# Weights split once in the first feed-forward part and reloaded as pairs, in a macaron block with a gated delta-rule attention

## The reference, cut to what matters

```python
x = x + 0.5 * ffn(layernorm(x))      # gate, up: 256 -> 768 (weights rounded to fp8), silu(gate)*up, down
x = x + attn(layernorm(x))
x = x + 0.5 * ffn(layernorm(x))

# attn: 16 heads of 128
q, k, v = silu(causal_conv4(x @ Wq)), silu(causal_conv4(x @ Wk)) * D**-0.5, silu(causal_conv4(x @ Wv))
alpha, beta = sigmoid(x @ Wa + ba), sigmoid(x @ Wb + bb)
def step(St, inp):                    # a scan over the tokens, per sequence and head
    q_, k_, v_, a_, b_ = inp
    err = einsum('bhij,bhj->bhi', St, k_) - v_
    Sn = a_ * St - b_ * err[..., None] * k_[..., None, :]
    return Sn, einsum('bhij,bhj->bhi', Sn, q_)
o = layernorm_per_head(scan(step)) * sigmoid(x @ Wg)
return o @ Wo
```

## Time and profile before

| | us |
|---|---|
| median of 3 runs | 2517.75 (2517.43 to 2521.06) |
| profiled execution, its own time | 2518.65 |
| its span, first to last instruction | 2516.9 |

### The profile page before, as it was taken

One profiled execution on the slowest core, in us unless ns is written; L12 is line 12 of the kernel. 1 busy time (PEld: TensorE's weight loads), 2 busy tenths in 40 slices (PEclk: granted clock), 3 DMA queues, 4 the chain that ended last, 5 costly groups with the idle time before them and its releaser, 6 DMA issues. The chain is left out here.

```text
span 2516.9 us, 64448 instructions
## 1 busy us (share of the span) xinstructions
PE 2364.4 (94%) x24496; PEld 1831.7 (73%) x24496; DVE 1989.7 (79%) x4226; ACT 1847.1 (73%) x3707; POOL 1873.3 (74%) x2057
## 2 busy tenths in 40 slices
PE   4996899999999999999998999999989999998598
PEld 2553688888777788888787888887778888887365
DVE  5654888888888788888887888888878888886353
ACT  2773677777888677777886777778867777776364
POOL 7762677777787777777886777778877777777365
PEclk8998999999999999999999999999999999999699
DMA  5000011111121111111211111112111111111001
GB/s 141 22 15 8 27 31 31 31 31 31 39 56 31 31 31 31 31 31 37 52 46 27 32 31 31 31 31 48 40 39 30 30 30 30 29 31 31 21 26 43
DMA packets 80609, 87.87 MB, mean 35 GB/s; under 512 B 21936, under 2 KB 50608, under 8 KB 80176
## 3 DMA queue, kind: packets, MB, share of 16 engines
q1 hardware_dynamic: 80304, 83.75, 13.9%
HBM read 77.83 MB, written 5.90 MB: 33 GB/s over the span
## 5 line engine op out<-in xcount | busy, mean ns | idle before, releaser
L1532 PE MATMUL a_bank<-k_z,k_kqv 128*128 128x512 f16 x2304 | 600.2, 381 | 11.2 <-DVE a_qb L1097 4.2
L1211 ACT ACTIVATE a_inv<-a_bank 128x512 f16<-128x512 f32 x640 | 382.9, 598 | 213.0 <-PE a_bank L1381 197.7
L1028 DVE TENSOR_TENSOR k_y<-a_bank,k_masks 128x256 f16<-128x256 f32 x768 | 318.5, 415 | 133.0 <-PE a_bank L1367 128.6
L1532 PEld LDWEIGHTS a_bank<-k_z,k_kqv 128*128 128x128 f16 x2304 | 198.5, 98 | 141.8 <-issue 19.5
L1097 DVE SCALAR_TENSOR_TENSOR a_kb<-a_bank,k_prm,a_kb 128x511 f32<-128x511 f32 (+2 forms) x384 | 282.8, 736 | 15.4 <-ACT a_kb L1155 15.0
L860 POOL TENSOR_TENSOR k_diag<-k_ident,k_bcol 128x512 f32<-128x512 f32 x128 | 133.0, 1039 | 215.0 <-DVE a_prod L1004 199.2
L1097 DVE SCALAR_TENSOR_TENSOR a_vb<-a_bank,k_prm,a_vb 128x511 f32<-128x511 f32 (+2 forms) x384 | 283.2, 738 | 0.1
L1097 DVE SCALAR_TENSOR_TENSOR a_qb<-a_bank,k_prm,a_qb 128x511 f32<-128x511 f32 (+2 forms) x384 | 282.4, 736 | 0.5
L1381 PE MATMUL a_bank<-a_inv,k_y 128*128 128x64 f16 x3072 | 272.0, 193 | 1.0 <-DVE k_y L1028 1.0
L1367 PEld LDWEIGHTS a_bank<-a_inv,a_am 128*128 128x128 f16 x3072 | 167.1, 98 | 105.8 <-ACT a_inv L1211 20.3
L1379 PE MATMUL a_bank<-k_y,a_inv 128*128 128x64 f16 x2560 | 236.6, 193 | 4.1 <-DVE k_y L1028 2.2
(11 more groups left out here) (151 smaller groups left out, 6778.3 us busy)
## 6 DMA issues: line engine op xcount, KB each, us to landing
a_decay<-decay_rows SPq DMA_DIRECT2D x128, 258.0 KB, 4.1
a_cum<-cumulative_rows SPq DMA_DIRECT2D x96, 258.0 KB, 3.6
stream<-in_L_attn_x SPq DMA_DIRECT2D x8, 512.0 KB, 6.8
out<-stream SPq DMA_DIRECT2D x8, 512.0 KB, 2.9
k_raw<-in_L_attn_Wk SPq DMA_DIRECT2D x16, 128.0 KB, 3.5
k_raw<-in_L_attn_Wq SPq DMA_DIRECT2D x16, 128.0 KB, 2.2
k_raw<-in_L_attn_Wv SPq DMA_DIRECT2D x16, 128.0 KB, 2.3
k_raw<-in_L_attn_Wg SPq DMA_DIRECT2D x16, 128.0 KB, 2.5
```

The costliest lines, as they stand in the source:

```text
L1028: nc.vector.tensor_tensor(even(y16[:, j], mb), bank[LEV[par]][:, 0:U * C // 2].rearrange("p (u b m) -> p u b m", u=U, m=mb), masks[:, j].r ...
L1211: nc.scalar.activation(both, bank[LEV[par]][:, :].rearrange("p (two b m) -> p two b m", two=2, m=mb), ACT.Copy).then_inc(m[f"act_lev{par}" ...
L1532: mm = pe.matmul(bank[PJ[j % 2]][:, :], wt, z16[:, zh, k, cols], start=(x == 0), stop=(x == 5))
```

## The change

All 16 heads' weights are split in the first feed-forward part. A part is now one kind of weight of one group, 128x1024 float32 (512 KB): 5 kinds times 4 groups are 20 parts, three in a turn from turn 1 on (`part_of`). SP loads a part into one of four raw buffers, ACT scales and rounds it in one instruction (`part_high`), DVE makes the low half in one (`part_low`). The parts of group 0 go straight to the tiles that the projections read; the other 15 go to one of two pair buffers, from which SP stores them to DRAM (`save_part`). In the attention the jobs are gone from ACT and POOL: SP loads a kind's pair, 512 KB, in one DMA each, five for a group, once the last projection with the old weights of that kind is done (`load_pairs`). Wo has two buffers, so its load does not wait for the last output. PE waits for the loads.

In the first feed-forward part the attention constants stand after turn 0 and the levels after turns 1 to 6, one in each (`level_constants`), both on POOL. ACT's turn begins four `silu` later, with the first ones ahead of the loop; DVE takes the statistics earlier and `hidden(b, 1)` into the turn; on PE `decay_products` stands earlier in the next turn, `strengths_turned` and `z_turned(1)` ahead of `down(b, 1)`, and `gate(b, 5)` after it. `root` counts on one semaphore in place of two. The last feed-forward part is as before but for that.

```diff
-JOBS = 4 * U + U
-SLOTS = 4
-WO_SLOTS = 1
-JOB_STEPS = {0: (0, 1, 2), 1: (3, 4, 5), 2: (6, 7, 8), 3: (9, 10, 11), 4: (12, 13, 14), 5: (15,)}
-OUT_STEPS = {8: (16, 17, 18, 19)}
-FIRST_JOB_STEP = -25
+KINDS = 5
+PARTS = KINDS * HG
+PART = KT * U * D
+RAW = 4
+PER_TURN = 3
+WO_SLOTS = 2
...
@@ first part: SP
+            def save_part(x):
+                if x is None:
+                    return
+                sp.wait_ge(d_part, x + 1)
+                if x >= KINDS:
+                    sp.dma_start(w_pairs[x], pairs[:, x % 2]).then_inc(s_pair[x % 2], 16)
+                if x + RAW < PARTS:
+                    load_part(x + RAW)
...
+                for x in range(RAW):
+                    load_part(x)
...
-                for job in range(6):
-                    load_job(nc, kit, w, sp, job)
-                for b in range(B):
-                    g = b % 2
-                    for job in range(3 * b + 6, min(3 * b + 9, JOBS)):
-                        load_job(nc, kit, w, sp, job)
-                    sp.wait_ge(d_ab, b + 1)
...
+                for t in range(1, B + 2):
+                    save_part(part_of(t, 0))
+                    store_rows(t - 2)
+                    save_part(part_of(t, 1))
+                    save_part(part_of(t, 2))
...
@@ first part: POOL
             def turn1(b):
                 low(b, 0)
                 root(1, b - 1)
                 low(b, 1)
-                weights(b, 0)
                 low(b, 2)
                 low(b, 3)
-                weights(b, 1)
+                root(0, b + 2)
                 low(b, 4)
                 low(b, 5)
-                root(0, b + 2)
-                weights(b, 2)
                 added(b)
...
                 root(0, 0)
-                attention_constants()
                 root(0, 1)
-                for b in range(0, B + 1):
+                for b in range(0, B + 2):
                     turn1(b)
+                    if b == 0:
+                        attention_constants()
+                    level_constants(b - 1)
...
@@ first part: DVE
+            def part_low(b, k):
+                x = part_of(b, k)
+                if x is None:
+                    return
+                dve.wait_ge(a_part, x + 1)
+                nc.vector.scalar_tensor_tensor(out=part_pair(x)[:, 1], in0=raw[:, x % RAW], scalar=WS,
+                                               in1=part_pair(x)[:, 0], op0=ALU.mult, op1=ALU.subtract)\
+                    .then_inc(d_part, 1)
...
             def turn1(b):
+                hidden(b, 1)
+                stats(1, b - 1)
                 hidden(b, 2)
+                part_low(b, 0)
+                hidden(b, 3)
                 logistic(b - 2)
+                stats(0, b + 2)
+                hidden(b, 4)
                 cumulative(b - 2)
-                hidden(b, 3)
                 strengths(b - 2)
-                hidden(b, 4)
                 low(1, b - 1)
                 hidden(b, 5)
-                stats(0, b + 2)
+                part_low(b, 1)
                 low(0, b + 1)
                 added(b)
+                part_low(b, 2)
                 hidden(b + 1, 0)
-                hidden(b + 1, 1)
-                stats(1, b)
...
@@ first part: ACT
+            def part_high(b, k):
+                x = part_of(b, k)
+                if x is None:
+                    return
+                act.wait_ge(s_part[x % RAW], 16 * (x // RAW + 1))
+                if x >= KINDS + 2:
+                    act.wait_ge(s_pair[x % 2], 16 * len(range(KINDS + (x - KINDS) % 2, x, 2)))
+                nc.scalar.activation(part_pair(x)[:, 0], raw[:, x % RAW], ACT.Copy, scale=WS).then_inc(a_part, 1)
...
             def turn1(b):
-                decays(b - 2)
-                silu(b, 0)
-                weights(b, 0)
-                silu(b, 1)
-                hidden_high(b, 0)
-                silu(b, 2)
-                normed(0, b + 1)
-                hidden_high(b, 1)
-                silu(b, 3)
-                hidden_high(b, 2)
-                weights(b, 1)
-                normed(1, b - 1)
                 silu(b, 4)
                 hidden_high(b, 3)
-                weights(b, 2)
                 high(1, b - 1)
+                hidden_high(b, 4)
                 silu(b, 5)
-                hidden_high(b, 4)
+                part_high(b, 2)
                 hidden_high(b, 5)
                 high(0, b + 1)
+                part_high(b + 1, 0)
+                normed(0, b + 2)
+                silu(b + 1, 0)
+                silu(b + 1, 1)
+                hidden_high(b + 1, 0)
+                part_high(b + 1, 1)
+                silu(b + 1, 2)
+                hidden_high(b + 1, 1)
+                silu(b + 1, 3)
+                hidden_high(b + 1, 2)
+                decays(b - 1)
+                normed(1, b)
...
+                normed(0, 1)
             act.wait_ge(s_small, 16 * (7 if first else 3))
             if first:
                 act.wait_ge(s_const, 8)
+            if first:
+                silu(0, 0)
+                silu(0, 1)
+                hidden_high(0, 0)
+                silu(0, 2)
+                hidden_high(0, 1)
+                silu(0, 3)
+                hidden_high(0, 2)
...
@@ first part: PE
                 gate(b, 3)
+                decay_products(b - 2)
                 up(b, 3)
+                gate(b, 4)
                 down(b, 0)
-                gate(b, 4)
                 up(b, 4)
+                strengths_turned(b - 2)
+                z_turned(1, b - 1)
+                down(b, 1)
                 gate(b, 5)
-                z_turned(1, b - 1)
-                strengths_turned(b - 2)
-                down(b, 1)
                 up(b, 5)
                 down(b, 2)
                 z_turned(0, b + 1)
-                decay_products(b - 1)
...
@@ attention: SP
+            def load_pairs(s):
+                group, kind = divmod(s - NC * (B - 1) + 2, NC * B)
+                group += 1
+                if kind >= KINDS or not 0 < group < HG:
+                    return
+                x = KINDS * group + kind
+                if kind < KINDS - 1:
+                    for j in range(U):
+                        sp.wait_ge(m[f"pe_pj{j}"], NC * (B * group - 1) + kind + 1)
+                else:
+                    need(sp, m["pe_wo"], NC * B * (group - WO_SLOTS + 1))
+                need(sp, m["dma_pairs"], 16 * (x - KINDS))
+                sp.dma_start(pair_tiles(kit, x), w_pairs[x]).then_inc(m["dma_pairs"], 16)
...
-                for job in jobs_of(s + 1) + jobs_of(s + 1, OUT_STEPS):
-                    load_job(nc, kit, w, sp, job)
+                load_pairs(s)
...
@@ attention: POOL and ACT
-            def weights(s):
-                for job in jobs_of(s - 2) + jobs_of(s - 1, OUT_STEPS):
-                    low_job(nc, kit, pool, job)
...
-                weights(s)
...
-            def weights(s):
-                for job in jobs_of(s - 1) + jobs_of(s - 1, OUT_STEPS):
...
@@ attention: PE
-                    pe.wait_ge(kit["pool_wl"], JOBS * (group + 1))
+                    need(pe, m["dma_pairs"], 16 * KINDS * group)
...
-                    if n % B == 0:
-                        pe.wait_ge(kit["pool_wl"], JOBS * (n // B) + U * i + j + 1)
+                    if n % B == 0 and j == 0 and n:
+                        pe.wait_ge(m["dma_pairs"], 16 * (KINDS * (n // B - 1) + i + 1))
...
-                    wt = gate16[:, wh, j, k] if i == 3 else kqv16[:, wh, i, j, k]
+                    wt = gate16[:, wh, k, j] if i == 3 else kqv16[:, wh, i, k, j]```

The order that follows from it, at three places. First ACT from its first silu (L528 before, L581 after) to the end of the products of turn 0; `f_sg` is the silu, `f_hh` the high half of the hidden values, `f_ztok` the normalised tokens, `k_raw` a weight tile. Before:

```order
5 L528 ACTIVATE f_sg<-f_bank,f_gs 128x512
6 L1623 ACTIVATE k_raw<-k_raw 128x256
7 L1625 ACTIVATE k_kqv<-k_raw 128x256
8 L528 ACTIVATE f_sg<-f_bank,f_gs 128x512
9 L537 ACTIVATE f_hh<-f_hid 128x512
10 L528 ACTIVATE f_sg<-f_bank,f_gs 128x512
11 L508 ACTIVATE f_ztok<-stream,f_shift,f_rstd 128x256 x4
12 L537 ACTIVATE f_hh<-f_hid 128x512
```

143 lines of the change are left out of this document (62 added, 81 removed).

## The result

The changed kernel takes 2474.37 us (median of 4 runs, 2473.62 to 2475.66), the kernel before, beside it, 2519.40 (2517.43 to 2521.45): a ratio of 0.9829, 95% interval 0.9817 to 0.984. The forecast was 2464.3, the range 2455 to 2475, so the result lies just inside its upper edge. The sign and the larger term were right; some 10 us were not won, and they are the subject of what follows. The profiled execution took 2475.66 us with a span of 2473.9.

What follows compares the result with a forecast made beforehand. The attention was taken as bound by PE except at three changes of group, which the weight jobs hold up. 2518.65 - 45.9 - (10 - 2.5 + 0) = 2465.2, with the median 0.9 lower: 2464.3 us, range 2455 to 2475.

Steps and rivals of the forecast that it cites:

- The attention, 45.9 us: Attention: removing the jobs wins the steps' whole excess, 45.9 us over 97 steps, 33.2 of it in three Wo steps.
- Loads of pairs, 0 us: Attention: 15 added loads of 512 KB land well inside over 25 us of room, so 0 is charged.
- Startup, 10 us won: First part, turn 0: it ends at 53.7 where it ended near 63.6, 10 us won.
- Turn 1, 23.4 us: First part: POOL's small constants make turn 1 take 23.4 us for 20.9, 2.5 us lost; bounds 0 and 5.
- Turns 2 to 7, 0 us: First part: six turns take 127.1 us in place of 127.2, 0 us; bounds -7 and +8.
- the one sentence on DVE: Turns 2 to 7: DVE's added 3 x 1.2 us stand in a turn with 8 us free, but ahead of the first `hidden`.
- the level on POOL: Turns 2 to 7: a level of 3.0 us for three jobs of 2.0, ahead of the root `normed(1)` waits for.
- The wait for stores, 1.4 us a turn in 4 to 6: First part: `part_high` waits for the store two parts back, 1.4 us of PE in each of turns 4 to 7; bounds 0 and 3.
- The rival "gives nothing back", 2472: First part: each `part_low` shuts POOL out for 1.2 us, six turns cost 7.5, startup's gain is gone: 2472; chance 0.2.
- One reading of the rows: Startup: four copies of a level took 4.71 us beside DVE's passes over two SBUF tensors, 1.14 us without them.

Runs made afterwards that it cites:

- the wait put back alone: Changed kernel with only POOL's wait for ACT put back in three steps, no work added: steps of 22.49, 23.0 and 23.27 us, 2494.7 us in the whole.
- low halves zero: Changed kernel with DVE writing zeros to each weight part's low half instead of subtracting: turns 2 to 7 126.0 us, whole 2464.95 us.
- the one with three buffers: Changed kernel with low halves written as zeros, and three pair and three raw buffers: turns 2 to 7 120.6 us, whole 2456.02 us.
- the three kernels with blocks of zeros: Changed kernel with zeros for the subtraction: written once 2464.95 us, written three times 2470.42 us, once with three pair and raw buffers 2456.02 us.
- the reordered kernel: Changed kernel with small constants before the first turn, third subtraction ahead of the scaling, levels' masks moved: 2466.15 us, ratio 0.9796.

## Why the prediction was right in the attention and wrong in the first part

- *The attention, 45.9 us:* measured 45.1 over the same 97 steps. Every step across a change of group is 16.0. The mechanism (the scaled q behind POOL's wait) holds by the wait put back alone.
- *Loads of pairs, 0 us:* they land in 4.7 to 6.0 us (medians by kind), and PE waits for none.
- *Startup, 10 us won:* 11.4, by the mechanism told: the first low half at 38.51 for 51.12. The sum had PE at the lower clock for 6 us from 37.85; it rose to 1.00 at 40.5, and with those 2.7 us the same sum ends turn 0 at 52.5 (measured: 52.37); with the rise at 43.6 (low halves zero) turn 0 ends at 53.74, nearly as forecast.
- *Turn 1, 23.4 us:* 24.1, but 22.6 at the full clock, so 1.7 us were lost against the 20.9 before, in place of 2.5. The cause was right: PE's two waits behind POOL make 4.6 of the 5.5 us charged, and the constants moved away take 3.2 us off. That 24.1 is so near to 23.4 is luck.
- *Turns 2 to 7, 0 us:* **this step failed**: 10.1 us lost, 11.7 at the full clock. The forecast of 20.7, 20.7, 21.7, 21.7, 21.7, 20.6 matches, nearly turn by turn, the kernel whose subtraction is a write of zeros: 20.3, 20.3, 21.7, 22.3, 21.7, 19.7. The term mis-sized most is the one sentence on DVE. Three times 1.2 us "in a turn that has 8 us free" were priced by the idle time of the whole turn. The subtractions stand in front of `hidden` and beside the root, and there they cost 11.3 us with their collisions. The second is the level on POOL, 3.0 us for jobs of 2.0, which got no time of its own in the sum though it "stands ahead of the root": without the levels the turns are 6.3 us shorter. The two costs overlap, since together they exceed the loss, and no run leaves out both.
- *The wait for stores, 1.4 us a turn in 4 to 6:* 1.6, 2.2 and 1.6 where the rest is out of the way (the zero kernel against the one with three buffers), and nothing where it is not.
- *The rival "gives nothing back", 2472:* this is what came. It charged six turns with 1.2 us each; they cost 1.7, and nearly 2 at the full clock. It had the rule right: the Trainium skill, "SBUF — State Buffer", section "Who interferes with whom", has GpSimd's reads shut out by a DVE instruction with two SBUF inputs but not by one with fewer, outside the modes in which it uses both ports. The trace agrees: L324, 0.20 us alone, takes up to 1.85 beside the subtraction and, in the first part, at most 0.49 in the three kernels with blocks of zeros. One reading of the rows was too wide: of the four copies that took 4.71 us in the kernel before, only one stood beside a pass over two tensors (1.73 us, from 25.72); the other three stood beside passes over one tensor and took 0.93 each, where undisturbed all four took 1.14. I gave it 0.2 on the ground that POOL was idle for 6 us a turn, which is again a share of a whole turn used for a question of place.
- *What two executions of one kernel differ by:* the places that differ by 1.4 to 1.7 us, in the turns, between the first and the fourth `a_at`, and at the end of the attention (2255.8 to 2259.1 us in the changed kernel), are stretches with the granted clock at 0.50. Why the clock falls behind one wait and not behind the same wait in another execution stays open.

## What to carry to other kernels

Work put on an engine with idle time is not free: ask which instruction it is queued ahead of, and what the other engine is doing at that moment. An instruction of 0.2 us on the path of a norm can pay for a whole subtraction elsewhere, and the row shows that as busy time, so compare its least and its most. Before a difference of 1 or 2 us is put down to an edit, compare the granted clock of the stretch. A wait whose removal gains nothing may only be hidden: here the buffers gained only once the order was mended. And a wait in an in-order queue is priced by what stands behind it: some 6 us of waiting on POOL, without work, cost 6.5 to 7.2 us a step, the lower clock behind it included.

## What the runs showed of the hardware that was not expected

POOL's steps are not the only ones to be held. DVE's scan over two SBUF tensors of 516 columns takes 1.21 us at the least (in the zero kernel) and 2.08 in the turn shown, begun beside POOL's low half at 137.98; and DVE's one-input L448 of the reordered kernel (L445 in the changed one, 32 x 512, f32 in place), otherwise 0.40 us, takes 1.18 beside POOL's low half at 128.14. The three copies of 0.93 us beside one-input passes, told above, show the same from POOL's side. So one input less is not always enough. The blocks of zeros in the scratch tile were never held, by their least, median and most:

```profile
L476 DVE MEMSET f_wexp<- x36: 485/485/485, 76.7 to 205.1; 128x512 uint32 x36
```
